# Scores in four column groups of the array, stacks without maximum padded with zero rows, and the products of two head groups in one bank

## The reference

```python
# L0_attn_b: queries and keys are softplus magnitudes times cos/sin, 16 numbers a head
scores = einsum('bhsd,bhtd->bhst', q_embed, k_embed) / D ** 0.5
out = einsum('bhst,bhtd->bhsd', softmax(scores), v)
# L1_attn_a: negative squared distances of the projected tokens, never above zero
scores = -(sq_norm - 2 * dot + sq_norm.T) * inv_sqrt_dk
context_q = einsum('bhst,bhtk->bhsk', softmax(scores), Q)
# L1_attn_b: scores plus a Gaussian gate -(j - P)**2 * 2 / Z**2
ctx = einsum('bhqk,bhkd->bhqd', softmax(q @ k.T / sqrt(D) + G), v)
```

## Time and profile before

| what | us |
|---|---|
| median of 3 runs (lowest, highest) | 1962.37 (1939.16, 1966.72) |
| the profiled execution, its own time | 1958.81 |
| its span in the trace | 1957.0 |
| mean granted TensorE clock | 0.912 |
| PE busy in the span | 1703.2 (87%) |
| ACT busy, DVE busy | 1319.0 (67%), 1265.4 (65%) |

### The profile page before, as it was taken

One profiled execution on the slowest core, in us unless ns is written; L12 is line 12 of the kernel. 1 busy time (PEld: TensorE's weight loads), 2 busy tenths in 40 slices (PEclk: granted clock), 3 DMA queues, 4 the chain that ended last, 5 costly groups with the idle time before them and its releaser, 6 DMA issues. The chain is left out here.

```text
span 1957.0 us, 30448 instructions
## 1 busy us (share of the span) xinstructions
PE 1703.2 (87%) x10142; PEld 725.4 (37%) x10142; DVE 1265.4 (65%) x2594; ACT 1319.0 (67%) x2222; POOL 347.9 (18%) x634
## 2 busy tenths in 40 slices
PE   7899976745999999978699999777764999999988
PEld 4666655620222222257222222245430222222256
DVE  4777786887999999745201111135556999999833
ACT  5555543971778777756459999656652878778863
POOL 4324223421000000033100000023321000000143
PEclk9998986975999999989759999889875999999999
DMA  4000000144222222100211111001233112212101
GB/s 116 1 1 1 1 1 1 49 148 127 67 75 75 67 73 75 37 1 25 80 38 53 50 50 50 8 17 56 73 91 90 53 53 58 60 53 55 38 7 38
DMA packets 114591, 98.49 MB, mean 50 GB/s; under 512 B 25866, under 2 KB 104516, under 8 KB 114436
## 3 DMA queue, kind: packets, MB, share of 16 engines
q1 hardware_dynamic: 112636, 95.61, 17.2%
q10 hardware_dynamic: 1800, 0.92, 0.2%
HBM read 64.34 MB, written 32.11 MB: 49 GB/s over the span
## 5 line engine op out<-in xcount | busy, mean ns | idle before, releaser
L1547 ACT ACTIVATE m_probs<-m_psum 128x512 f32<-128x512 f32 (+1 forms) x768 | 525.5, 740 | 167.1 <-PE m_psum L1455 156.8
L1547 ACT ACTIVATE e_probs<-e_psum 128x512 f32<-128x512 f32 x512 | 277.6, 599 | 93.6 <-PE e_psum L1455 84.4
L1587 DVE TENSOR_REDUCE a_minus_max<-e_psum 128x1 f32<-128x512 f32 x512 | 317.3, 683 | 24.6 <-PE e_psum L1464 24.5
L1587 DVE TENSOR_REDUCE a_minus_max<-m_psum 128x1 f32<-128x512 f32 x512 | 317.3, 683 | 23.7 <-PE m_psum L1464 23.6
L1455 PE MATMUL m_psum<-m_q_stack,m_k_stack 114*128 114x512 bf16 (+1 forms) x1024 | 301.6, 398 | 10.4 <-DMA m_k_stack<-n_parts 8.3
L1475 PE MATMUL m_psum<-m_probs,m_v_ones 128*16 128x512 f32 x2048 | 283.4, 622 | 1.4 <-ACT m_probs L1547 1.2
L1455 PEld LDWEIGHTS m_psum<-m_q_stack,m_k_stack 114*128 114x128 bf16 (+1 forms) x1024 | 72.7, 98 | 258.1 <-ACT m_probs L1547 150.3
L1455 PE MATMUL e_psum<-e_q_stack,e_k_stack 126*128 126x512 bf16 x512 | 156.0, 387 | 2.1 <-ACT e_probs L1547 2.1
L1475 PE MATMUL e_psum<-e_probs,e_v_ones 128*16 128x512 f32 x1024 | 136.6, 597 | 0.9 <-POOL e_v_ones L1421 0.7
L1428 POOL CAST a_max_parts<-a_minus_max 128x16 bf16<-128x16 f32 x64 | 12.7, 198 | 681.4 <-DVE a_minus_max L1587 681.4
L1464 PE MATMUL m_psum<-m_k_stack,m_q_stack 48*128 48x512 bf16 x512 | 100.1, 401 | 35.3 <-DMA m_k_stack<-polar_k 34.7
(11 more groups left out here) (392 smaller groups left out, 2809.7 us busy)
## 6 DMA issues: line engine op xcount, KB each, us to landing
polar_q<-d_p_q_parts SPq DMA_DIRECT2D x24, 256.0 KB, 3.1
polar_k<-d_p_k_parts SPq DMA_DIRECT2D x24, 256.0 KB, 3.2
m_q_stack<-polar_q SPq DMA_DIRECT2D x64, 96.0 KB
m_q_stack<-dist_parts SPq DMA_DIRECT2D x192, 32.0 KB
m_k_stack<-dist_parts SPq DMA_DIRECT2D x192, 32.0 KB
gate_parts<-d_p_curve_parts SPq DMA_DIRECT2D x24, 256.0 KB, 3.0
m_k_stack<-polar_k SPq DMA_DIRECT2D x62, 96.0 KB
e_q_stack<-gate_parts SPq DMA_DIRECT2D x64, 72.0 KB
```

What stands on the lines that cost most here:

```text
L1547: act.activation(self.buf.probs[(NT * m + c) % self.buf.PROBS][:, self.WIDE * part:self.WIDE * (part + 1), :], self.ps_s[i % self.PAIRS], ...
L1587: dve.tensor_reduce(self.minus_max[n % 2][:, k:k + 1], ps[:, :], AX.X, ALU.max, negate=True).then_inc(self.bank_free, 1)
```

## The change

1. `unit`: each 128-column score product becomes four products of 32 key columns, each into its own 32 partitions of the same bank, in one column group of the array each. The moving data is the same 512 queries. One wait and one increment a unit as before.
2. Without maximum (a5) the stacks are used with 66 rows in place of 54: the 12 added rows of the key stack are zero. `fill_keys` there becomes three memsets a slot and a wait between them.
3. `pv` multiplies by 32 columns: the values of even steps stand in columns 0 to 15 of one buffer, those of odd steps in 16 to 31 of the other, zeros elsewhere. Two steps accumulate into the bank, `start` only in the even one, `stop` only in the odd one.
4. The evacuation, the four transposes and the division happen once for two steps, after the odd one. The reciprocal is of 128x32, and two multiplications follow.
5. The ring has fewer uses, so the banks that the next phase takes over are the last four uses whatever they are.

```diff
-    VW = 16
+    VW = 2 * 16
...
-            last = pool.memset(self.v_ones[u][:, :, :, DH:DH + 1], 1.0)
+            last = pool.memset(self.v_ones[u][:, :, :, 16 * u + DH:16 * u + DH + 1], 1.0)
...
-        self.rows = self.max_at + 2 if self.with_max else rows
+        self.PAD = 0 if self.with_max else 12
+        self.rows = self.max_at + 2 if self.with_max else rows + self.PAD
...
-                if c == 2 and s - self.LAG >= 1:
+                if c == 2 and s - self.LAG >= 1 and (s - self.LAG) % 2 == 0:
                     uses.append(("ctx", s - self.LAG - 1))
...
-            last = pe.matmul(self.ps_s[i % self.PAIRS][:, j, :], self.buf.k_stack[g][0:self.rows, h, c * P:(c + 1) * P],
-                             self.buf.q_stack[g][0:self.rows, h, :], start=True, stop=True)
+            for r in range(0, P, 32):
+                last = pe.matmul(self.ps_s[i % self.PAIRS][r:r + 32, j, :], self.buf.k_stack[g][0:self.rows, h, c * P + r:c * P + r + 32],
+                                 self.buf.q_stack[g][0:self.rows, h, :], start=True, stop=True)
...
-            wait_ge(pe, self.ctxT_ready, m)
+            wait_ge(pe, self.ctxT_ready, m // 2)
...
-                             self.buf.probs[(NT * m + c) % self.buf.PROBS][:, h, :], start=(c == 0), stop=(c == NT - 1))
+                             self.buf.probs[(NT * m + c) % self.buf.PROBS][:, h, :], start=(c == 0 and m % 2 == 0), stop=(c == NT - 1 and m % 2 == 1))
...
-            if c == 2 and m >= 1:
+            if c == 2 and m >= 1 and m % 2 == 0:
                 self.turn_ctx(pe, m - 1)
...
-            if self.with_max and v == self.PER and m >= 1:
+            if self.with_max and v == self.PER and m >= 1 and m % 2 == 0:
                 self.evacuate(act, m - 1)
...
-                last = dve.memset(buf.k_stack[u][32:self.rows, :, :].bitcast(F32), self.ONES)
+                dve.memset(buf.k_stack[u][64:self.rows, :, :].bitcast(F32), 0.0)
+                dve.memset(buf.k_stack[u][32:64, :, :].bitcast(F32), 0.0).then_inc(self.zeroed, 1)
+                dve.wait_ge(self.zeroed, u + 1)
+                last = dve.memset(buf.k_stack[u][32:self.rows - self.PAD, :, :].bitcast(F32), self.ONES)
...
-        dve.tensor_tensor(self.sv.ctx[:, tiles_of(b), g * GW:(g + 1) * GW].rearrange("p t (h d) -> p t h d", h=GH),
-                          raw[:, :, :, 0:DH], over(inv[:, :, :], P, NT, GH, DH), ALU.mult).then_inc(self.bank_free, 1)
+        for u in range(2):
+            first = (g - 1 + u) * GW
+            last = dve.tensor_tensor(self.sv.ctx[:, tiles_of(b), first:first + GW].rearrange("p t (h d) -> p t h d", h=GH),
+                                     raw[:, :, :, u, 0:DH], over(inv[:, :, :, u], P, NT, GH, DH), ALU.mult)
+        last.then_inc(self.bank_free, 1)
...
-            if not self.with_max and c == 0 and s >= 1:
+            if not self.with_max and c == 0 and s >= 1 and s % 2 == 0:
                 self.evacuate(dve, s - 1)
-            if c == 2 and s - self.LAG >= 1:
+            if c == 2 and s - self.LAG >= 1 and (s - self.LAG) % 2 == 0:
                 self.normalise(dve, s - self.LAG - 1)
```

More of the change, by code:

```diff
@@ L901, in __init__ @@
         ffn = self.ffn = Experts(nc, sv, f"{tag}_f", norm)
-        self.place = (before.ring_place(("max", NB * NG - 1)), before.scores[0], before.ring_place(("ctx", NB * NG - 3)),
-                      before.ring_place(("ctx", NB * NG - 2)), before.ring_place(("ctx", NB * NG - 1)), before.scores[1], before.scores[2], before.pv_place)
+        free = [before.ring_place(use) for use in before.last_uses]
+        self.place = (free[0], before.scores[0], free[1], free[2], free[3], before.scores[1], before.scores[2], before.pv_place)
         prep = self.prep = PrepareDistance(nc, sv, f"{tag}_p", norm2, psum[:, self.place[7], :], before)
@@ L1199, in __init__ @@
         self.bo_added, self.stored = nc.alloc_semaphore(f"{tag}_bo_added"), nc.alloc_semaphore(f"{tag}_stored")
-        self.place = (before.ring_place(("max", NB * NG - 1)), before.ring_place(("ctx", NB * NG - 2)), before.ring_place(("ctx", NB * NG - 3)),
-                      before.scores[0], before.scores[1], before.scores[2], before.pv_place, before.ring_place(("ctx", NB * NG - 1)))
+        free = [before.ring_place(use) for use in before.last_uses]
+        self.place = (free[0], free[2], free[1], before.scores[0], before.scores[1], before.scores[2], before.pv_place, free[3])
         banks = self.banks = Banks(nc, tag, 8, (
@@ L1292, in __init__ @@
         self.ctxT = [sb(f"ctxT{u}", [P, T]) for u in range(2)]
-        self.inv = [sb(f"inv{u}", [P, NT, GH]) for u in range(2)]
+        self.inv = [sb(f"inv{u}", [P, NT, GH, 2]) for u in range(2)]
         self.prepared = nc.alloc_semaphore(f"{tag}_prepared")
@@ L1337, in sem @@
             return nc.alloc_semaphore(f"{tag}_{name}")
+        self.zeroed = sem("zeroed")
         self.bank_zeroed, self.filled, self.loaded = sem("bank_zeroed"), [sem(f"filled{u}") for u in range(buf.SLOTS)], [sem(f"loaded{u}") for u in range(buf.SLOTS)]
@@ L1357, in __init__ @@
         self.nth = {use: r for r, use in enumerate(uses)}
+        self.last_uses = uses[-self.BANKS:]
     def ring_place(self, use):
@@ L1367, in bank_done @@
         elif place == self.pv_place:
-            eng.wait_ge(self.ctxT_ready, self.N)
+            eng.wait_ge(self.ctxT_ready, self.N // 2)
         else:
@@ L1420, in copy_v @@
             self.before.values_ready(pool, b)
-        pool.tensor_copy(self.buf.v_ones[n % 2][:, :, :, 0:DH],
+        pool.tensor_copy(self.buf.v_ones[n % 2][:, :, :, 16 * (n % 2):16 * (n % 2) + DH],
                          self.sv.vtok[:, tiles_of(b), g * GW:(g + 1) * GW].rearrange("p t (h d) -> p t h d", h=GH)).then_inc(self.v_copied, 1)
@@ L1475, in pv @@
             last = pe.matmul(self.ps_pv[32 * h:32 * h + self.buf.VW, :], self.buf.v_ones[m % 2][:, c, h, :],
-                             self.buf.probs[(NT * m + c) % self.buf.PROBS][:, h, :], start=(c == 0), stop=(c == NT - 1))
+                             self.buf.probs[(NT * m + c) % self.buf.PROBS][:, h, :], start=(c == 0 and m % 2 == 0), stop=(c == NT - 1 and m % 2 == 1))
         last.then_inc(self.pv_done, 1)
     def turn_ctx(self, pe, m):
-        pe.wait_ge(self.ctxT_ready, m + 1)
+        pe.wait_ge(self.ctxT_ready, m // 2 + 1)
         to = self.bank(pe, ("ctx", m))
         for t in range(NT):
-            last = pe.transpose(to[:, t * P:(t + 1) * P], self.buf.ctxT[m % 2][:, t * P:(t + 1) * P], self.sv.ident[:, :])
+            last = pe.transpose(to[:, t * P:(t + 1) * P], self.buf.ctxT[m // 2 % 2][:, t * P:(t + 1) * P], self.sv.ident[:, :])
         last.then_inc(self.bank_full, 1)
@@ L1531, in evacuate @@
         eng.wait_ge(self.pv_done, NT * m + NT)
-        if m >= 2:
-            eng.wait_ge(self.bank_full, self.nth["ctx", m - 2] + 1)
+        if m >= 4:
+            eng.wait_ge(self.bank_full, self.nth["ctx", m - 4] + 1)
         if self.with_max:
-            copied = eng.activation(self.buf.ctxT[m % 2][:, :], self.ps_pv[:, :], ACT.Copy)
+            copied = eng.activation(self.buf.ctxT[m // 2 % 2][:, :], self.ps_pv[:, :], ACT.Copy)
         else:
-            copied = eng.tensor_copy(self.buf.ctxT[m % 2][:, :], self.ps_pv[:, :])
+            copied = eng.tensor_copy(self.buf.ctxT[m // 2 % 2][:, :], self.ps_pv[:, :])
         copied.then_inc(self.ctxT_ready, 1)
@@ L1595, in normalise @@
         b, g = divmod(m, NG)
[L1596 to L1599, removed]
+        raw = self.full(dve, ("ctx", m))[:, :].rearrange("p (t h u c) -> p t h u c", t=NT, h=GH, u=2)
+        inv = self.buf.inv[m // 2 % 2]
+        dve.reciprocal(inv[:, :, :, :], raw[:, :, :, :, DH]).then_inc(self.inv_ready, 1)
+        dve.wait_ge(self.inv_ready, m // 2 + 1)
         if self.before is not None:
             self.before.context_used(dve, b)
-        dve.tensor_tensor(self.sv.ctx[:, tiles_of(b), g * GW:(g + 1) * GW].rearrange("p t (h d) -> p t h d", h=GH),
-                          raw[:, :, :, 0:DH], over(inv[:, :, :], P, NT, GH, DH), ALU.mult).then_inc(self.bank_free, 1)
+        for u in range(2):
[3 more added lines that the diff above has]
+        last.then_inc(self.bank_free, 1)
     def vector(self, dve, s):
```

## The result

The changed kernel takes 1887.38 us (median of 4 runs, 1885.93 to 1892.29) against 1961.91 for the kernel before measured beside it: ratio 0.965, 95% interval 0.957 to 0.972. The prediction was 1880, range 1848 to 1947. The profiled execution took 1887.1 with a span of 1885.3, 71.7 less than the 1957.0 of before.

What follows compares the result with a forecast made beforehand. PE was taken as full in all loops, with DVE close behind in a3 and ACT in a5. Terms -40 (a3, a7), -28 (a5), +9 (memsets), -21 (clock) sum to -80 from 1958.8: 1879, predicted 1880, range 1848 to 1947.

Steps and rivals of the forecast that it cites:

- a3 and a7: -40 forecast: Loops a3 and a7: 0.44 a step from drains plus 0.18 from turning the context half as often, -40 us in all.
- The drains between units and `pv`: PE in a3 and a7: 0.11 and 0.12 us vanish, 0.22 a chunk; half shows, chunk 2.67 to 2.565.
- The model of two legs over two chunks: a3 and a7: PE's 2.87 and DVE's 2.48 us together span two chunks, so half of PE's saving shows.
- the turned context: a3 and a7: about 0.68 us every second step, 0.34 a step, saving 0.18 a step.
- a5: -28 and -21 forecast: Loop a5: step 8.38 to 7.5 us with ACT next to bind, -28; earlier release from half clock, -21.
- The clock term: Start of a5: either no change (0) or release from half clock within 10 to 15 us (-21); the second was taken.
- Fills: +9 forecast: Head of DVE's queue in DistancePhase: eight more memsets for a5 at 1.1 us each, from 0 to 9, taken as +9.
- Covered by nothing that I can name: DVE, DistancePhase: said of the first added memsets, to explain taking the full +9 us.
- SP's queue: Loads and maxima transfers in a3: 1.1 us of the step may go before this path binds; at 0.62 it does not.
- rival 2: Column groups of bf16 don't fully overlap: four quarter products take 0.27 in place of 0.216, total 1947; 10%.
- rival 3: PE's instruction supply binds in a3 and a5: 1983 at 47 ns an instruction, 2347 at 64 ns; 12%.
- rival 4: Clock lost: a5 stays at half clock to the end, steps of 14.2 us, total 2083; 6%.

Runs made afterwards that it cites:

- the shorter reductions: The changed kernel with row maxima taken over 480 of the 512 keys in a3 and a7: 1878.53 us, 11.6 below the changed kernel beside it.
- the spread fills: The changed kernel with two memsets a slot, one slot at the end of each of four DistancePhase steps: 1879.63 us, ratio to before 0.961.

## Why the prediction was right

**The bound.** PE full, DVE and ACT close behind: so it was, and both took over what PE gave up.

**a3 and a7: -40 forecast, -35 measured.** The drains between units and `pv` went, 0.11 and 0.12, and half of them shows: a chunk is 2.56 where 2.565 was forecast, and that term stands. The model of two legs over two chunks is what the shorter reductions test from DVE's side, and they move the chunk by half. A step is 10.84 (21.68 for two, 701.30 to 722.98 in PE's timeline) for 10.76 forecast. The term that was mis-sized is the turned context, 0.68 every second step by the prediction. Four chunks without it are 722.98 - 712.55 = 10.43, so the two steps hold 21.68 - 20.86 = 0.82 for it (PE's timeline, tiles at the head of three steps):

```profile
701.30 0.78 PE L1468 MATMUL m_psum<-m_k_stack,m_q_stack 48*128 48x512 bf16 x4
...
712.55 0.78 PE L1468 MATMUL m_psum<-m_k_stack,m_q_stack 48*128 48x512 bf16 x4
...
722.98 0.78 PE L1468 MATMUL m_psum<-m_k_stack,m_q_stack 48*128 48x512 bf16 x4
```

The difference, 0.07 a step, is 4.5 us over both loops, nearly the whole miss. I kept 0.49 for it on PE and left out that its neighbours become another kind: 0.59 (706.58 - 705.99). Also two products and a wider reciprocal occupy DVE for 707.55 - 706.71 = 0.84 where it was 0.75. How the 0.14 divides between the two isn't shown. The kernel with whole scores and the shared bank shows the halving alone at 2 us a loop, not 6.

**a5: -28 and -21 forecast, -47.6 measured.** The step is 7.63, not 7.5: ACT's gap at the turned context is 0.49 where I took 0.25, and 8.39 - 7.63 over 32 steps is 24. The other 24 or so are the clock: 56.5 us at half clock became 5.7, half of the difference is 25. So one term was 4 us too large and the other 3 too small, and that their sum fits is luck. The clock term was also a choice between 0 and -21 that the rows could not decide, as the prediction says. Its support was thinner than it reads: a7's "released after 9.5" counts from 1508.0, but a7's first tile starts at 1493.9, and the clock reads 0.50 from there to 1517.5, for 23.6 us in which PE is busy for 22.94. The reasons given were rows, whole groups and drains. The runs bear out the rows, as far as single profiled executions can: 114 rows end the stretch with the drains in place. At 66 rows it ends only in the kernels with quarter products and no drains (40.0 against 7.3 and 5.7), and 16 columns of `v_ones` do as well as 32.

**Fills: +9 forecast.** The twelve memsets hold DVE from 844.53 to 858.34, 13.8 us, where the four held it for 4.1: 9.7 more. The pair of profiles gives +13.8 for d5, the means over all kernels 9.6, the spread fills 11. "Covered by nothing that I can name" was right while they stood together, and spreading them finds the cover.

**The rest.** d7's -3.1 lies inside its scatter of 233.7 to 240.3 over the kernels. SP's queue did not bind: between 600 and 780 SP still waited 40.8 us in 17 places for the scores, 2.4 a step.

**The rivals.** Four column groups of bf16 do overlap fully here. PE's timeline in a5 after, against the earlier trace rows:

```profile
1101.51 1.07 PE L1459 MATMUL m_psum<-m_q_stack,m_k_stack 66*32 66x512 bf16 x16
1102.37 1.07 PE L1479 MATMUL m_psum<-m_probs,m_v_ones 128*32 128x512 f32 x8
```

Sixteen quarter products take 1102.37 - 1101.51 = 0.86 without a drain, 0.215 for four, so the 0.27 of rival 2 is out. The Trainium skill gives 2.38x for three column tiles (TensorE: Matmul & The Clock Gate, Part 3, Measured speedup vs the span model); this trace does not agree with it as a rate of a stream. PE's instruction supply (rival 3) kept up with 16 loads and 16 products in that 0.86, 27 ns each, and over a5's whole step, 200 in 7.63, 38 ns each, both below the 47 of the densest longer row that I had. The clock (rival 4) went the other way.

## What to carry to other kernels

Count the changes of the kind of product (row span and column span of the array) in PE's order and price each from the timeline, 0.11 us here: a product cut into column groups costs nothing in streaming and can be made the same kind as its neighbours, with zero rows if need be, but whatever keeps the old kind between them, such as a transpose, then pays at both ends. Where two engines hand banks back and forth over two chunks, expect about half of what either saves. The work added at the head of DVE's queue in a phase of short steps cost its full length here, some 10 us; spread over the steps' ends it did not show.

## What the runs showed of the hardware that I had not expected

A PE that is 100% busy by the profile can stay at half clock for 40 to 70 us: seven forms of this loop were released after 5.5 to 69.7 us, and rows that hold only zeros in the weights made a difference (the table above). That zero rows help at all, 56.5 to 5.5 us with 114 rows, was new to me. The two kernels with 54 rows and the shared bank also had runs 30 to 130 us longer than their shortest, at a lower granted clock.

PE's order mattered more than its sum: moving one unit behind the products with `v_ones`, and one behind the tiles, cost 15 us. A wait for ACT's copy of the context is about half of it; the rest is open.
